# Bias-then-mix kernel: stores begun on SyncE in 4-tile pieces, three loads of x a region, bias units of one tile

## Chip, cores and metric

One core of one Trainium2 chip. The metric is the device time of one execution in microseconds (us), all engines and transfers included. Engines are named as in the profile: PE (TensorE matmul), PEld (its weight load), DVE (VectorE), ACT (ScalarE), POOL (GpSimd), SP (SyncE). "SPq" and "ACTq" are the DMA-issuing instructions of SP and ACT.

## The reference, cut to what matters

```python
# x: (1, 16 heads, 1024 rows t, 1024 columns s), float32
rel  = tril(t - s)                                   # distance, 0 above the diagonal
nd   = log(|c*rel| + 1) / (log(|c*max(t, threshold)| + 1) + EPS)
h    = relu(nd[..., None] * W1[0] + b1)              # 32 hidden values for each (t, s)
y    = x + (h @ W2 + b2)                             # a bias for each head, t, s
out[n,t,s] = sum over m of y[m,t,s] * (A[t][m,n] + B[s][m,n])
# A[t] = w + I + two rank-one terms of qw1, qw2 + diag(qdd): one 16x16 matrix for each row
# B[s] = two rank-one terms of kw1, kw2 + diag(kdd): one 16x16 matrix for each column
```

## The kernel before, in words

x and out are 67 MB each and cross the DMA once each. The 128 partitions hold 16 heads of 8 blocks of 128 columns. A **tile** is 8 rows (all heads, all columns, 512 KB); there are 128. A **region** is a stretch of tiles that is worked on together: region 0 has 8 tiles, regions 1 to 10 have 12 each. Three SBUF areas ("homes") of 13 tile slots take turns: one holds y of region k, one x of region k+1 while it becomes y, one the mixed output of region k, which is stored and then gives its place to x of region k+2.

A region k runs through 16 **column steps** (C = 0 to 15; each mixes 8 columns of every block over all rows of the region with B, `b_columns`, line 750, 64-row weights in 4 places of the array) and then one **row step** for each tile T (`a_rows`, line 735, with A). Steps are numbered s = 0 to 15 and 16 to 27. The matmul results go to one of two PSUM buffers, `main`. In column steps ACT empties the even ones and DVE the odd ones into the mixed home (`take_b`, lines 534 and 636, three copies each; in region 0 ACT takes all). In row steps DVE adds the tile to what lies there (`finish_tile`, line 647). Two fp32 records of the profile are one matmul.

The **bias** of region k+1 is made during region k, at the steps that `BIAS_STEPS` lists. Before, a unit is 16 rows (two tiles): ACT makes `hidden` (line 516) in pieces of 4 blocks, four activations of up to 512 columns for each piece, into a ring of two pieces; PE multiplies it with W2 (`bias_unit`, line 766, 32x32 places, 512 columns, as many output quadrants as lie below the diagonal: 1 for rows 0 to 255, up to 4 for the last 256) into the four PSUM banks of `bias`, which exist once; DVE adds the bias to x, tile by tile, at the unit's step and the next (`add_bias`, line 663, two halves of 512 columns, after a wait for the load of x). Units of a 12-tile region stand at steps 3, 9, 15, 18, 21 and 24. A unit with three or four quadrants is two pieces, the whole ring, so its successor's activations wait until PE has used it (line 512). PE waits in turn for all `hidden` of a unit, and for `y_ready` of the tile before.

Engines run their own program in order, written out by hand; semaphores join them. What sets the order of the DMAs:
- **Stores** (`store_block`, line 313): a region of 12 tiles is stored in pieces of 2, 3, 3 and 4 tiles. Of the 8 blocks of a piece ACT begins four, two at each of two steps behind the last tile of the piece (`portions_at`, line 549 on), and SP the other four.
- **Loads of x** (`load_x`, line 359): pieces of 1, 3, 3, 3 and 2 tiles, 8 DMAs each, all on SP. A piece waits (in SP's program, `out_done`) until the stores that free its slots have landed. Pieces 0, 1 and 2 of region k+2 stand at T = 6, 9 and 11 of region k, the last two behind them, ahead of everything of region k+1.
- **A matrices** (`load_mats_a`, line 367): 4 DMAs for 32 rows, on SP at every fourth tile; POOL spreads them (line 453) after a wait for PE's row steps.

A row of a block is 128 columns of 4 bytes, so x and out move in runs of 512 bytes.

Of the kernel before, what the change touches and what calls it, by code (L numbers as in the profile page):

```python
# [46 lines left out]
BIAS_ROWS = 16  # L47
BIAS_TILES = BIAS_ROWS // ROWS
BIAS_UNITS = S // BIAS_ROWS
SLOT_ROWS = BIAS_ROWS // SLOTS  # L50
PIECE_BLOCKS = 4
PIECE = PIECE_BLOCKS * SLOT_ROWS * W
# [13 lines left out]
def build(nc, x, W1, b1, W2, b2, c, L_mult, init_L, qw1, qw2, kw1, kw2, qdd, kdd, w, out):  # L66
# [5 lines left out]
    with ExitStack() as ctx:  # L72
# [16 lines left out]
        hidden = sb("hidden", [P, RING, PIECE])  # L89
        log_table = sb("log_table", [P, TABLE])  # L90
        row_scale = sb("row_scale", [P, BIAS_UNITS * SLOT_ROWS])
# [64 lines left out]
        def quadrants_of(v):  # L156
            return v * BIAS_ROWS // (QB * W) + 1

        def pieces_of(v):

            blocks = QB * quadrants_of(v)
            return [(b, min(b + PIECE_BLOCKS, blocks)) for b in range(0, blocks, PIECE_BLOCKS)]

        def piece_index(v, i):
            return sum(len(pieces_of(w)) for w in range(v)) + i

        def unit_of_piece(h):
            return max(v for v in range(BIAS_UNITS) if piece_index(v, 0) <= h)

        def hidden_rows(v, i):  # L170
            return hidden[:, piece_index(v, i) % RING, :].rearrange("p (b j s) -> p b j s", j=SLOT_ROWS, s=W)

# [19 lines left out]
        def bias_step(k, n):  # L192

            return BIAS_STEPS[REGION_TILES[k]][n]

        def bias_unit_at(k, s):
            if k + 1 < REGIONS:
                for n in range(REGION_TILES[k + 1] // BIAS_TILES):
                    if bias_step(k, n) == s:
                        return n  # L200
            return None

        def bias_tile_at(k, s):

            n, before = bias_unit_at(k, s), bias_unit_at(k, s - 1)
            if n is not None:
                return n * BIAS_TILES
            return before * BIAS_TILES + 1 if before is not None else None

        def first_unit(k):  # L210
            return FIRST_TILE[k] // BIAS_TILES

        def hidden_parts(v):
            return [(i, j) for i in range(len(pieces_of(v))) for j in range(SLOT_ROWS)]

        def hidden_parts_at(k, s):

            if k + 1 == REGIONS:
                return []
            found = []  # L220
            for n in range(REGION_TILES[k + 1] // BIAS_TILES):
                begun = bias_step(k, n - 1) if n else bias_step(k, 0) - 2
                room = bias_step(k, n) - begun
                parts = hidden_parts(first_unit(k + 1) + n)
                for x, part in enumerate(parts):
                    if begun + x * room // len(parts) == s:
                        found.append((first_unit(k + 1) + n, part))
            return found
# [90 lines left out]
        def portions_at(k, s):  # L319

            found = []
            for r, step in ((k - 1, s + REGION_TILES[k - 1] if k else -1), (k, s - COL_TILES)):
                if r < 0:
                    continue
                for i in range(len(store_pieces(r))):
                    p = step - piece_start(store_pieces(r), i + 1)
                    if 0 <= p < len(PORTIONS):
                        found.append((r, i, p))
            return found

# [13 lines left out]
        def _(sp):  # L344
# [7 lines left out]
            def load_x(k, i):  # L352
                T, n = piece_start(load_pieces(k), i), load_pieces(k)[i]
                if k >= 2 and T + 1 < REGION_TILES[k - 2]:
                    left = piece_of(store_pieces(k - 2), min(T + n, REGION_TILES[k - 2] - 1))
                    sp.wait_ge(out_done[left], times(store_pieces, left, k - 2) * PER_PIECE)
# [126 lines left out]
        def _(act):  # L483
# [20 lines left out]
            def make_hidden(v, part):  # L504
# [14 lines left out]
                if j == SLOT_ROWS - 1:  # L519
                    made.then_inc(hidden_ready, 1)  # L520
# [289 lines left out]
```

## Time and profile before

| | |
|---|---|
| median of 3 runs | 829.97 us (827.63 to 835.9) |
| the profiled execution | 834.87 us; its span, first to last instruction, 833.1 us |
| mean granted TensorE clock | 0.868 of full |
| busy share of the span | PE 70%, DVE 58%, ACT 48%, POOL 19% |
| DMA | 148.37 MB, mean 178 GB/s |

How to read it: times in the rows are us from the span's start unless marked ns. "x32" behind a row is the number of instructions that it merges. The number in square brackets is idle time of that engine just before, and what ended it. The DMA share is the mean busy share of the core's 16 DMA engines. A releaser is inferred from semaphores. The start of a region is read from PE's first column matmuls (a merged row of `mats_b` matmuls right after the last of `mats_a`).

### The profile page before, as it was taken

The page shows a single profiled execution, that of the slowest core. Times are in us where ns is not written, and L with a number is a line of the kernel's source. Part 1 is how long each engine was busy: PE and PEld are TensorE (multiplying, and loading weights), DVE is VectorE, ACT ScalarE, POOL GpSimd, SP SyncE. Part 2 cuts the span into 40 slices and gives each one's busy share as a digit, 9 for nine tenths or more (in the row PEclk, how much of TensorE's full clock was granted, in tenths as well). Part 3 has the DMA queues.
Part 4 walks back from the last instruction along what each step waited for, and adds up shares of the span by engine and source line. Part 5 has one row for each costly group of instructions (what it writes and reads, how often), then busy time and mean ns, then how long its engine had stood idle before and what let it go on. Part 6 is the DMA issues. An engine that isn't in the chain of part 4 may idle for free. (4 is left out here: it accounts for less than half of the span.)

```text
span 833.1 us, 27560 instructions
## 1 busy us (share of the span) xinstructions
PE 581.9 (70%) x12336; PEld 429.0 (51%) x12336; DVE 484.6 (58%) x648; ACT 399.0 (48%) x683; POOL 158.0 (19%) x156
## 2 busy tenths in 40 slices
PE   0556853884896598389569858955974795779683
PEld 0133632663574366167446636834762474357583
DVE  5482633782684577268366746826673475467463
ACT  3548341415523442454385366457537573574310
POOL 1092410130031023003102200400220031003020
PEclk9758985996897799789799989978997799799797
DMA  6978689579879969887986997898599768868739
GB/s 125 212 174 156 156 173 201 123 187 209 186 181 201 198 146 200 183 181 181 225 203 139 201 224 168 184 211 184 135 208 208 156 143 203 184 151 175 143 73 232
DMA packets 298914, 148.37 MB, mean 178 GB/s; under 512 B 30252, under 2 KB 294572, under 8 KB 298668
## 3 DMA queue, kind: packets, MB, share of 16 engines
q1 hardware_dynamic: 229360, 113.03, 61.7%
q10 hardware_dynamic: 69436, 33.58, 17.5%
q8 instruction: 97, 1.59, 0.9%
q14 instruction: 21, 0.17, 0.1%
HBM read 77.34 MB, written 69.21 MB: 176 GB/s over the span
## 5 line engine op out<-in xcount | busy, mean ns | idle before, releaser
L516 ACT ACTIVATE hidden<-log_table,b_col,row_scale 128x512 f32<-128x512 f32 (+1 forms) x384 | 258.0, 734 | 152.6 <-PE bias L766 87.0
L663 DVE SCALAR_TENSOR_TENSOR homes<-bias,b_col,homes 128x512 f32<-128x512 f32 x256 | 180.1, 746 | 205.3 <-PE bias L766 159.3
L750 PE MATMUL main<-homes,mats_b 64*64 64x96 f32 (+1 forms) x5632 | 174.5, 274 | 137.6 <-DVE homes L636 65.6
L735 PEld LDWEIGHTS main<-homes,mats_a 64*64 64x64 f32 x4096 | 231.4, 132 | 35.7 <-issue 29.0
L453 POOL TENSOR_TENSOR mats_a<-mats_in,own_block 128x512 f32<-128x512 f32 x128 | 130.6, 1042 | 617.3 <-PE main L735 601.9
L750 PEld LDWEIGHTS main<-homes,mats_b 64*64 64x64 f32 x5632 | 148.0, 154 | 188.0 <-DVE homes L636 73.7
L534 ACT ACTIVATE homes<-main 64x384 f32<-64x384 f32 (+3 forms) x288 | 134.2, 466 | 229.1 <-PE main L750 209.0
L735 PE MATMUL main<-homes,mats_a 64*64 64x128 f32 x4096 | 241.9, 273 | 0.6 <-issue 0.3
L766 PE MATMUL bias<-hidden,w_blocks 32*32 32x512 f32 x2560 | 166.7, 719 | 88.0 <-ACT hidden L516 71.0
L636 DVE COPY homes<-main 64x384 f32<-64x384 f32 (+1 forms) x240 | 133.2, 555 | 98.0 <-PE main L750 95.8
L647 DVE TENSOR_TENSOR homes<-main,homes 128x1024 f32<-128x1024 f32 x128 | 154.2, 1221 | 25.7 <-PE main L735 25.6
L766 PEld LDWEIGHTS bias<-hidden,w_blocks 32*32 32x32 f32 x2560 | 45.0, 114 | 152.0 <-issue 130.1
L453 POOL TENSOR_TENSOR mats_b<-homes,own_block 128x512 f32<-128x512 f32 x16 | 24.3, 1554 | 38.6 <-DMA homes<-b_mats 38.6
L700 PE MATMUL bias<-relu_b,w_blocks 32*32 32x1 f32 x16 | 0.4, 191 | 12.1 <-DVE w_blocks L619 12.1
L335 DVE TENSOR_TENSOR homes<-mats_in 128x2048 f32<-128x2048 f32 x3 | 8.4, 2826 | 0.0
L700 PEld LDWEIGHTS bias<-relu_b,w_blocks 32*32 32x32 f32 x16 | 0.3, 144 | 12.1 <-issue 12.1
L543 ACT ACTIVATE bias<-zero_col,const_col 32x2048 f32<-32x2048 f32 (+1 forms) x2 | 3.9, 1964 | 5.5 <-DVE const_col L629 5.5
L692 PEld LDWEIGHTS main<-homes 128*128 128x128 f32 x32 | 4.3, 163 | 3.1 <-DVE homes L609 1.7
L495 ACT ACT_TABLE_LOAD x1 | 1.3, 1283 | 7.5 <-issue 7.5
L692 PE MATMUL main<-homes 128*128 128x128 f32 x32 | 4.7, 311 | 0.0
L526 ACT ACTIVATE homes<-main 128x1024 f32<-128x1024 f32 x2 | 1.9, 1023 | 4.0 <-PE main L692 4.0
L607 DVE TENSOR_TENSOR homes<-homes 128x2048 f32<-128x2048 f32 x1 | 3.0, 3014 | 0.0
(32 smaller groups left out, 21.7 us busy)
## 6 DMA issues: line engine op xcount, KB each, us to landing
homes<-in_x SPq DMA_DIRECT2D x248, 192.0 KB, 6.2
out_mixed<-homes ACTq DMA_DIRECT2D x88, 192.0 KB
out_mixed<-homes SPq DMA_DIRECT2D x88, 192.0 KB
homes<-in_x SPq DMA_DIRECT2D x80, 128.0 KB, 4.4
out_mixed<-homes ACTq DMA_DIRECT2D x36, 256.0 KB, 6.9
out_mixed<-homes SPq DMA_DIRECT2D x36, 256.0 KB, 6.2
mats_in<-a_mats SPq DMA_DIRECT2D x128, 64.0 KB, 3.4
out_mixed<-homes SPq DMA_DIRECT2D x48, 128.0 KB, 3.9
```

Of the source, the lines that this page charges most:

```text
L335: return eng.tensor_tensor(dst.rearrange("p (b m n) -> p b m n", b=BLOCKS, m=H), u.unsqueeze(3).to_broadcast(shape), v.unsqueeze(2).to_bro ...
L453: return nc.gpsimd.tensor_tensor(sums.rearrange("p e (n b) -> p e n b", b=QB), rows.rearrange("p n e -> p e n").unsqueeze(3).to_broadcast( ...
L516: made = nc.scalar.activation(hidden_rows(v, i)[:, 0:end_block - first_block, j, :], logs.rearrange("p (b s) -> p b s", s=W), ACT.Relu, bi ...
L534: copy = nc.scalar.activation(mixed_columns(into, k, C, part), column_sums(of, k, C, part), ACT.Copy)
L543: fill = nc.scalar.activation(bias[into].rearrange("p q s -> p (q s)"), zero_col[into].to_broadcast([into.stop - into.start, SLOTS * BANK] ...
L636: copy = dve.tensor_copy(mixed_columns(into, k, C, part), column_sums(of, k, C, part))
L647: dve.tensor_tensor(at, main[:, i % 2, :], at, ALU.add).then_inc(main_taken[i % 2], 1)
L663: add = dve.scalar_tensor_tensor(out=y_rows(whole, k, T, b), in0=falling(u, b), scalar=b2_col[:, 0:1], in1=x_rows(whole, k, T, b), op0=ALU ...
L692: mm = pe.transpose(main[:, i % 2, b * P:(b + 1) * P], comp[part][:, at:at + P], ident)
L735: mm = pe.matmul(main[of_group(g), i % 2, j * W:(j + 1) * W], a_weights(g, w, part * ROWS + j), y_row(k, T, g, j), start=True, stop=True)
L750: mm = pe.matmul(main[into, i % 2, j * W:j * W + REGION_TILES[k] * ROWS], b_weights(g, C * ROWS + j), y_column(k, g, C * ROWS + j), start= ...
L766: mm = pe.matmul(bias[of_quadrant(into), q, :], w2_blocks[of_quadrant(q), b, :], rows, start=b == 0, stop=b == QB - 1)
```

## The change

- Stores: pieces of 4 tiles (8-tile region: 4, 4; 12-tile: 4, 4, 4). All 8 blocks of a piece are begun on SP, in one go, as soon as the piece's last tile is finished. Only the last region keeps its six pieces (2, 3, 3, 2, 1, 1) shared by SP and ACT.
- Loads of x: 3 pieces of 3, 4 and 5 tiles. In SP's program those of region k+2 stand behind the stores of region k: the first behind the second store, the other two behind the third.
- Bias: a unit is one tile (8 rows). Its `hidden` is two activations of all blocks at once (256 to 1024 columns), the ring holds two tiles, the matmuls have 256 columns instead of 512 and there are as many of them for a tile as before for two. In a 12-tile region the tiles stand at steps 4, 8, 12, 15 and then 16, 17, 18, 20, 21, 22, 23, 24, each with its own addition on DVE at the same step.

SP's program for a region of 12 tiles is then: at T=3 store piece 0, A chunk; at T=7 store piece 1, A chunk, x piece 0 of region k+2; at T=11 store piece 2, A chunk, x pieces 1 and 2.

```diff
-STORE_PIECES = {8: (2, 3, 3), 12: (2, 3, 3, 4)}
+STORE_PIECES = {8: (4, 4), 12: (4, 4, 4)}
-LOAD_PIECES = {8: (1, 3, 4), 12: (1, 3, 3, 3, 2)}
-X_PIECES = 5
+LOAD_PIECES = {8: (1, 3, 4), 12: (3, 4, 5)}
+X_PIECES = 3
-BIAS_STEPS = {8: (3, 8, 12, 15, 18, 20), 12: (3, 9, 15, 18, 21, 24)}
+BIAS_STEPS = {8: (2, 4, 6, 8, 10, 12, 14, 16, 17, 18, 20, 21), 12: (4, 8, 12, 15, 16, 17, 18, 20, 21, 22, 23, 24)}
-BIAS_ROWS = 16
...
-SLOT_ROWS = BIAS_ROWS // SLOTS
-PIECE_BLOCKS = 4
-PIECE = PIECE_BLOCKS * SLOT_ROWS * W
+SLOT_ROWS = ROWS // SLOTS
+HIDDEN = BLOCKS * SLOT_ROWS * W
 RING = 2
...
+            for T, step in enumerate(bias_steps(k)):
+                begun = bias_steps(k)[T - 1] if T else step - 2
+                for j in range(SLOT_ROWS):
+                    if begun + j * (step - begun) // SLOT_ROWS == s:
+                        found.append((tile_of(k + 1, T), j))
             return found
...
+        def is_shared(k, i):
+
+            return k + 1 == REGIONS
...
+        def stores_before(k, i):
+
+            T, n = piece_start(load_pieces(k), i), load_pieces(k)[i]
+            if k < 2 or T + 1 >= REGION_TILES[k - 2]:
+                return None
+            return piece_of(store_pieces(k - 2), min(T + n, REGION_TILES[k - 2] - 1))
...
-            def store_upper(k, i):
+            def store_piece(k, i):
                 taken, count = emptied(a_tile(k, piece_start(store_pieces(k), i + 1) - 1))
                 sp.wait_ge(taken, count)
-                for b in BLOCK_ORDER[sum(PORTIONS):]:
+                for b in BLOCK_ORDER[sum(PORTIONS):] if is_shared(k, i) else BLOCK_ORDER:
                     store_block(sp, k, i, b).then_inc(out_done[i], DMA)
...
-            for i in range(3):
+            for i in range(X_PIECES - 1):
                 load_x(1, i)
             save_mats("a")
-            load_x(1, 3)
             sp.wait_ge(mats_out["a"], 2 * DMA)
             for v in range(A_RING):
                 load_mats_a(v)
-            load_x(1, 4)
-            loaded = [3, X_PIECES] + [0] * (REGIONS - 2)
+            load_x(1, X_PIECES - 1)
             for k in range(REGIONS):
-
-                while k + 1 < REGIONS and loaded[k + 1] < X_PIECES:
-                    load_x(k + 1, loaded[k + 1])
-                    loaded[k + 1] += 1
+                pieces, loaded = store_pieces(k), 0
                 for T in range(REGION_TILES[k]):
+                    stored = [i for i in range(len(pieces)) if T == piece_start(pieces, i + 1) - 1]
+                    for i in stored:
+                        store_piece(k, i)
                     v = chunk_behind(tile_of(k, T))
                     if v is not None:
                         load_mats_a(v)
-                    for i in range(len(store_pieces(k))):
-                        if T == piece_start(store_pieces(k), i + 1) - 1 - (i == 3 and k < REGIONS - 1):
-                            store_upper(k, i)
-                    if k + 2 < REGIONS and T in (6, 9, 11):
-                        load_x(k + 2, loaded[k + 2])
-                        loaded[k + 2] += 1
+                    for i in stored:
+
+                        while k + 2 < REGIONS and loaded < X_PIECES and (
+                                i + 1 == len(pieces) or stores_before(k + 2, loaded) < i):
+                            load_x(k + 2, loaded)
+                            loaded += 1
...
+            def make_hidden(u, j):
+                blocks = QB * quadrants_of(u)
...
+                if j == 0 and u >= RING:
+                    act.wait_ge(hidden_used, u - RING + 1)
+                at = u * ROWS + j - (blocks * W - 1) + BEFORE
+                made = nc.scalar.activation(hidden_rows(u)[:, 0:blocks, j, :],
...
-            def falling(u, b):
-                at = (u % BIAS_TILES) * 2 + b
-                return bass.AP(bias, at * BANK + W - 1, [[SLOTS * BANK, P], [W, SLOT_ROWS], [-1, W]])
+            def falling(b):
+                return bass.AP(bias, b * W + W - 1, [[SLOTS * BANK, P], [BANK, SLOTS], [-1, W]])
...
-                dve.wait_ge(hidden_used, u // BIAS_TILES + 1)
+                dve.wait_ge(hidden_used, u + 1)
...
+            def bias_tile(u):
+                if u:
+                    pe.wait_ge(y_ready, u)
+                pe.wait_ge(hidden_ready, u + 1)
                 for b in range(QB):
                     for q in range(SLOTS):
+                        for into in range(quadrants_of(u)):
+                            at = QB * quadrants_of(u) - 1 - (QB * into + b)
+                            mm = pe.matmul(bias[of_quadrant(into), q, 0:SLOT_ROWS * W], w2_blocks[of_quadrant(q), b, :],
+                                           hidden_rows(u)[of_quadrant(q), at], start=b == 0, stop=b == QB - 1)
                 mm.then_inc(hidden_used, 1)
```

## Rows read from the trace of the kernel before

**Rows 1.** Waits: engine, tile, line <- releaser: us in total, times, longest us
```profile
ACT hidden L516 <- PE bias L766: 87.0, 27, 4.5
...
PE bias L766 <- ACT hidden L516: 71.0, 31, 8.3
...
DVE homes L663 <- DMA homes<-in_x: 40.2, 7, 14.5
```

**Rows 2.** Busy time by stage: PE, PEld, DVE, ACT, POOL busy; PEclk, DMA share, GB/s
```profile
183.20:225.20 42.00, 24.68 (x608) 16.38 (x608) 19.90 (x33) 22.59 (x39) 2.05 (x2) 0.76 0.93 198
...
695.20:739.90 44.70, 24.55 (x704) 15.24 (x704) 20.00 (x34) 29.00 (x48) 2.04 (x2) 0.85 0.90 207
739.90:771.20 31.30, 29.48 (x582) 24.24 (x576) 23.80 (x28) 17.38 (x24) 10.21 (x10) 1.00 0.66 144
```

**Rows 3.** Timeline of PE, regions 9 and 10: start us, us, work [idle before <-releaser]
```profile
699.70 1.56 PE L750 MATMUL main<-homes,mats_b 64*64 64x96 f32 x64 [2.33 <-ACT homes L534]
708.71 3.75 PE L766 MATMUL bias<-hidden,w_blocks 32*32 32x512 f32 x64 [7.46 <-ACT hidden L516]
...
723.02 4.08 PE L766 MATMUL bias<-hidden,w_blocks 32*32 32x512 f32 x64 [2.14 <-ACT hidden L516]
...
739.93 5.66 PE L735 MATMUL main<-homes,mats_a 64*64 64x128 f32 x96
745.93 2.34 PE L766 MATMUL bias<-hidden,w_blocks 32*32 32x512 f32 x64 [0.35 <-ACT hidden L516]
...
771.37 0.90 PE L750 MATMUL main<-homes,mats_b 64*64 64x96 f32 x32 [0.24 <-DVE homes L647]
...
797.95 22.25 PE L735 MATMUL main<-homes,mats_a 64*64 64x128 f32 x384
```

**Rows 4.** Timeline of ACT, regions 0 and 9
```profile
85.67 2.08 ACT L516 ACTIVATE hidden<-log_table,b_col,row_scale 128x256 f32<-128x256 f32 x4
...
689.27 8.84 ACTq L313 DMA_DIRECT2D out_mixed<-homes  x4
...
704.16 1.46 ACT L534 ACTIVATE homes<-main 128x384 f32<-128x384 f32 x3
...
740.03 5.75 ACT L516 ACTIVATE hidden<-log_table,b_col,row_scale 128x512 f32<-128x512 f32 x8 [2.52 <-PE bias L766]
```

**Rows 5.** Timeline of DVE, region 9
```profile
720.95 1.69 DVE L636 COPY homes<-main 128x384 f32<-128x384 f32 x3 [1.02 <-PE main L750]
727.23 2.91 DVE L663 SCALAR_TENSOR_TENSOR homes<-bias,b_col,homes 128x512 f32<-128x512 f32 x4 [4.58 <-PE bias L766]
...
742.10 1.23 DVE L647 TENSOR_TENSOR homes<-main,homes 128x1024 f32<-128x1024 f32 x1 [0.56 <-PE main L735]
```

**Rows 6.** Timeline of PE, regions 0 to 4: other widths and region starts
```profile
61.39 0.70 PE L750 MATMUL main<-homes,mats_b 64*64 64x64 f32 x32 [0.24 <-ACT homes L526]
...
106.44 0.90 PE L750 MATMUL main<-homes,mats_b 64*64 64x96 f32 x32 [0.24 <-DVE homes L647]
...
168.09 1.92 PE L766 MATMUL bias<-hidden,w_blocks 32*32 32x512 f32 x16
...
183.28 0.90 PE L750 MATMUL main<-homes,mats_b 64*64 64x96 f32 x32 [0.24 <-DVE homes L647]
...
230.90 1.95 PE L766 MATMUL bias<-hidden,w_blocks 32*32 32x512 f32 x32
...
384.35 2.21 PE L766 MATMUL bias<-hidden,w_blocks 32*32 32x512 f32 x48
```

**Rows 7.** The page's DMA queues: packets, MB, share of 16 engines' span
```profile
q1 hardware_dynamic: 229360, 113.03, 61.7%
q10 hardware_dynamic: 69436, 33.58, 17.5%
```

**Rows 8.** Timeline of SyncE's issues, three loads of x in a row
```profile
492.30 19.37 SPq L359 DMA_DIRECT2D homes<-in_x  x24
```

**Rows 9.** The loads of x (line 359), from issue to landing
```profile
DMA to landing us min/median/max: 3.4/5.8/9.0
```

More of the change, by code:

```diff
@@ L154, in tile_of, with quadrants_of, hidden_rows @@
             return FIRST_TILE[k] + T
[L156 to L171, printed above, removed]
+        def quadrants_of(u):
+            return u * ROWS // (QB * W) + 1
+        def hidden_rows(u):
+            return hidden[:, u % RING, :].rearrange("p (b j s) -> p b j s", j=SLOT_ROWS, s=W)
         def turned_tile(part, half):
@@ L190, in emptied, with bias_steps @@
             return main_taken[i % 2], i // 2 + 1
[L192 to L201, printed above, removed]
-        def bias_tile_at(k, s):
[L205 to L214, printed above, removed]
+        def bias_steps(k):
+            return BIAS_STEPS[REGION_TILES[k]] if k + 1 < REGIONS else ()
+        def bias_tile_at(k, s):
+            return bias_steps(k).index(s) if s in bias_steps(k) else None
         def hidden_parts_at(k, s):
-            if k + 1 == REGIONS:
-                return []
             found = []
[L221 to L227, printed above, removed]
+            for T, step in enumerate(bias_steps(k)):
[3 more added lines that the diff above has]
+                        found.append((tile_of(k + 1, T), j))
             return found
@@ L317, in portion_blocks, with portions_at @@
             return BLOCK_ORDER[sum(PORTIONS[:p]):sum(PORTIONS[:p + 1])]
-        def portions_at(k, s):
+        def is_shared(k, i):
+            return k + 1 == REGIONS
+        def portions_at(k, step):
             found = []
[L322 to L328, printed above, removed]
-            return found
+            for i in range(len(store_pieces(k))):
+                p = step - piece_start(store_pieces(k), i + 1)
+                if is_shared(k, i) and 0 <= p < len(PORTIONS):
+                    found.append((i, p))
+            return found
+        def stores_before(k, i):
[3 more added lines that the diff above has]
+            return piece_of(store_pieces(k - 2), min(T + n, REGION_TILES[k - 2] - 1))
         def rank_one(eng, part, i, dst):
@@ L353, in load_x @@
                 T, n = piece_start(load_pieces(k), i), load_pieces(k)[i]
-                if k >= 2 and T + 1 < REGION_TILES[k - 2]:
-                    left = piece_of(store_pieces(k - 2), min(T + n, REGION_TILES[k - 2] - 1))
+                left = stores_before(k, i)
+                if left is not None:
                     sp.wait_ge(out_done[left], times(store_pieces, left, k - 2) * PER_PIECE)
@@ L535, in take_b @@
                 copy.then_inc(main_taken[b_tile(k, C) % 2], 1)
-            for v in range(REGION_TILES[0] // BIAS_TILES):
-                for part in hidden_parts(v):
-                    make_hidden(v, part)
-                if v == 0:
+            for u in range(REGION_TILES[0]):
+                for j in range(SLOT_ROWS):
+                    make_hidden(u, j)
+                if u == 0:
                     act.wait_ge(const_bias_read, 1)
@@ L546, in _ @@
                     fill.then_inc(const_filled, 1)
-                if v == 1:
+                if u == 2:
                     take_turned("b")
@@ L550, in _ @@
                 for s in steps(k):
[L551 to L556 removed]
+                    for i, p in portions_at(k, s - COL_TILES):
+                        store_portion(k, i, p)
                     if s == TURN_AT and k == 0:
@@ L560, in _ @@
                         take_b(k, s)
-                    for v, part in hidden_parts_at(k, s):
-                        make_hidden(v, part)
-            r = REGIONS - 1
-            for i in range(len(store_pieces(r))):
-                for p in range(len(PORTIONS)):
-                    if piece_start(store_pieces(REGIONS - 1), i + 1) + p >= REGION_TILES[REGIONS - 1]:
-                        if p == 0:
-                            taken, count = emptied(a_tile(REGIONS - 1, piece_start(store_pieces(REGIONS - 1), i + 1) - 1))
-                            act.wait_ge(taken, count)
-                        for b in portion_blocks(p):
-                            store_block(act, REGIONS - 1, i, b).then_inc(out_done[i], DMA)
+                    for u, j in hidden_parts_at(k, s):
+                        make_hidden(u, j)
+            for step in range(REGION_TILES[REGIONS - 1], REGION_TILES[REGIONS - 1] + len(PORTIONS)):
+                for i, p in portions_at(REGIONS - 1, step):
+                    store_portion(REGIONS - 1, i, p)
         @block.vector
```

62 lines of the change are left out of this document (21 added, 41 removed).

## The prediction

> **What bounds the kernel now.** I read the waits first: ACT's `hidden` waits on PE's bias matmuls and these on `hidden`, 87.0 and 71.0 us [rows 1]. That is one loop: a unit with three or four quadrants fills the whole ring, so ACT and PE work in turn. Next the stages: in region 9 the column steps take 44.5 us, in which PE is busy 24.5 and ACT 29.0, and the row steps 31.3, in which PE is busy 29.5 [rows 2]. The column steps are thus where time is lost, the row steps are PE's. PE's timeline shows the loss: 7.46 and 2.14 us idle before bias units, a third wait like the second, units of 3.75 and 4.08 us behind such waits against 2.34 in the row steps, and 2.33 us at the start, when ACT is late [rows 3] because it sits in 8.84 us of DMA issues [rows 4]. Last the DMA: both queues' packets take 61.7 + 17.5 = 79.2% of 833.1 us for 146.6 MB, that is 4.50 us/MB or 222 GB/s at full share [rows 7]. The column steps run at 198 and 207 GB/s with a share of 0.90 to 0.93, the row steps at 144 [rows 2]. So the DMA is the second bound, close behind, and the question is how soon it becomes the first.
>
> **Prices.** A row tile is 5.66/3 or 22.25/12, 1.87 us [rows 3]. A column step is 0.90 on PE [rows 3]; a pair goes round in DVE's 1.69 plus the 1.02 in which DVE waits for the same buffer, 2.71 [rows 5]. ACT's three copies are 1.46 [rows 4], DVE's addition of one tile 1.41 to 1.46 (2.91 for two) and `finish_tile` 1.23 [rows 5].
>
> **`hidden`.** 256 columns cost 2.08/4 = 0.52, 512 cost 5.75/8 = 0.72 [rows 4]; 0.20 for 256 columns gives 0.92 for 768 and 1.12 for 1024, so 2.24 us a tile at most against 2.88 for half a unit before. Bounds of the 1024: 0.72 and twice that. At 1.12 ACT's column pair is 1.46 + 1.12 = 2.58, inside DVE's 2.71; at 1.44 it would be 2.90, and 8 pairs cost 1.5 us more. In the row steps ACT needs 2.24 for a step of 3.3 on PE, and the ring of two tiles lets it run ahead. So the loop of [rows 1] goes, and 0 of `hidden` is left on the path. ACT's issues fall from 180 stores to 24, so its late start in each column stage goes too.
>
> **Bias matmuls with 256 columns.** The trace has none. A unit of 512 columns is 1.92, 1.95, 2.21 and 2.34 us for 16, 32, 48 and 64 records [rows 3, 6]. Lower end: half. Upper end: no cheaper than 512, since the count stays. Between them: 32 records of the column steps take 0.90 with 96 columns and 0.70 with 64 [rows 3, 6], so 0.30 of 32 records does not depend on columns, 9 ns a record. With that a tile of 64 records is 0.6 + (2.34 - 0.6)/2 = 1.47; for 16, 32, 48: 1.03, 1.12, 1.32. I take 1.0, 1.1, 1.3, 1.45 for one to four quadrants. Two tiles cost PE up to 0.6 more than the unit did.
>
> **Column stage after.** Start and first pair 1.1, 7 pairs x 2.71 = 19.0, the last step 0.9: 21.0. Three tiles (steps 4, 8, 12) each put an addition of 1.41 into DVE's round, with some wait for PE about 1.5: 4.5. Bias of T=3 behind step 15: 1.1. Sum 26.6; I take 27 at two quadrants, 27.4 at three, 28 at four, where 40 to 48 stand now.
>
> **Row stage after.** 12 x 1.87 + 8 tiles x 1.1 = 31.2 at two quadrants, 32.8 at three, 34 at four (DVE's 1.23 + 1.41 = 2.64 fits into a step of 2.95). Without a DMA wait a region would take 58.5 to 62.5 us.
>
> **The DMA after.** A region moves 12 x 0.524 MB twice and 3 x 0.262 of A: 13.37 MB, at 4.50 us/MB 60.2 us. One store piece is 9.4, an A chunk 1.2, the loads 7.1, 9.4, 11.8. All of it is in SP's order now. SP can issue that fast: 24 loads, 4.72 MB, in 19.37 us, 244 GB/s [rows 8]. What counts is where x lands. Let e be the region's end; its T=7 is finished at e - 8.3 (four more tiles and a bias; two quadrants). Behind that come store 1, A, x piece 0: e - 8.3 + 9.5 + 1.2 + 7.1 = e + 9.5, and about 3 for landing (3.4 is the shortest of issue to landing [rows 9]): e + 12.5. The next region wants this x for its T=0 behind step 4, at e + 7.6. So DVE waits 4.9 us, every region, with the empty column copies of DVE queued behind this wait, and PE behind them; another 1.5 goes as PE comes back slow (a unit behind a wait costs 3.75 against 2.34 [rows 3]). Piece 1 lands at e + 9.5 + 9.5 + 1.2 + 9.5 + 3 = e + 32.7, wanted at step 15, e + 33; piece 2 at e + 44.5, wanted at step 20, e + 47. They fit, barely. The queue is then empty for some 4 us until the next store at T=3.
> A region of two quadrants: 0.2 + 27 + 4.9 + 1.5 + 31.1 = 64.7; three: 65.9; four: 67.4 (the wait shrinks to 4 as the rows lengthen). 13.37 MB in 64.7 us is 207 GB/s, what region 9's column stage moves now [rows 2].
>
> A rule of the Trainium skill bears on the stores (DMA: Bandwidth & Descriptors, section "Issuing engines are not separate DMA queues"): transfers begun on several engines run on the same 16 DMA engines, so a second issuing engine saves only issue time. By it the move to SP neither gains nor loses bandwidth. The same page (section "Queues, rings and completion order") says that a DMA engine takes packets from its queues in turn; with one queue a load gets no turn ahead of a store. The trace has SP's loads at full rate alone, but no stretch with all stores on SP, so it does not settle that; the 4.9 us already hold the full delay.
>
> **Regions 0, 1 and 10.** Region 0 keeps its setup; its tail gains 2 us from five single tiles and a later x piece. Region 1 takes 183.28 - 106.44 = 76.8 us now [rows 6] with its wait for x, the longest of 14.5 [rows 1]. After, region 0's two stores follow its T=3 and T=7, so x piece 0 of region 2 lands at about 131 (T=7 at 109, then 1.3 behind store 0, 9.5, 1.2, 7.1, 3) and is wanted at 116: 15 us again, and region 1 ends at 183 as before. Regions 2 to 9 run from 183.3 to 771.4, 588.1 us [rows 3, 6]; after: 3 x 64.7 + 2 x 65.9 + 3 x 67.4 = 528. Region 10 has no bias; its column stage, 797.95 - 771.37 = 26.6 [rows 3], falls to 8 x 2.71 + 1 = 22.7 since ACT is not late; row steps and last stores stay. Sum: 833.1 - 60 - 4 = 769 us of span. The profiled execution was 834.87 for 833.1, so 771 for this one; the median 829.97 is 0.994 of it: **766 us**.
>
> **Rivals.**
> 1. *The DMA does not bind.* If the packets got shorter with traffic of one kind at a time, x would be there at step 4. For it: three loads at 244 GB/s [rows 8]. Against: 4.50 us/MB over the run [rows 7]. Regions of 58.3, 60 and 62.5 make 482, less 10 in region 1: about 712. The Trainium skill (DMA: Bandwidth & Descriptors, section "Specifications") gives a limit of some 358 GB/s for each core from HBM; at that, an estimate, 13.37 MB would take 37 us. No run here shows such a rate.
> 2. *256 columns cost what 512 cost.* Then bias tiles are 1.9 to 2.3, a region has 12 x 0.8 more on PE, of which the wait at step 4 gives back 2.4: 7 us x 8, about 822. Against: the slope between 64 and 96 columns [rows 3, 6].
> 3. *Slower: one queue, one order.* Stores and loads take turns in a single queue, and x piece 0 waits behind a whole store. At a rate r a region is 13.37 MB/r and 4 us of empty queue; the present 73.5 is reached at 192 GB/s. For it: 198 GB/s in region 2's column stage at a share of 0.93 [rows 2]. Against: 222 at full share [rows 7]. At 181 GB/s, 6% below that, a region is 78, 8 x 78 = 624, the whole 862.
>
> **Numbers.** Forecast 0.74, with its own range 741 to 804: the DMA between 235 and 200 GB/s moves a region's traffic by 3.3 down and 6.6 up, of which I let half show since PE is close behind; bias tiles and `hidden` towards their bounds are 1.5 either way; 8 regions x -3.2 and +4.8. Rival 1: 0.08; rival 2: 0.08, half of it within 1%; rival 3: 0.10, nearly all slower by over 1%. One per cent is about what a measurement of this kernel can tell. So faster 0.74 + 0.08 + 0.04 = 0.86, same 0.05, slower 0.09. The range 735 to 815 leaves out most of rival 1 and 3 and part of 2.
>
> **What would show it.** Right: ACT `hidden` and PE bias hardly wait for each other; bias matmuls near 1.0 to 1.5 us a tile; column stages of 30 to 34 us with one DVE wait of some 5 us on x at step 4; DMA share above 0.9 throughout regions 2 to 9, at 205 to 215 GB/s. Wrong: DVE waits on x also at steps 15 and 20; row steps above 35 us; a DMA rate below 195 GB/s with a share near 1.

## The result and the profile after

The change makes the kernel slower: 888.62 us against 832.41 in the same comparison, a ratio of 1.069 (95% interval 1.063 to 1.075). The profiled execution took 886.17 us for a span of 884.4. Medians in this document are over all executions of a kernel; ratios and their intervals leave out those in a second, slower state, in which the profiles of the kernel before and of `e12_pairs_from_2` were taken.

The page of the kernel after (engine totals; queues: packets, MB, share of 16 engines' span; chain by engine):

```profile
PE 617.0 (70%) x14896; PEld 476.2 (54%) x14896; DVE 490.9 (56%) x648; ACT 367.9 (42%) x555; POOL 158.6 (18%) x156
...
q1 hardware_dynamic: 287408, 143.44, 79.9%
q10 hardware_dynamic: 7548, 3.16, 1.6%
q8 instruction: 117, 1.92, 1.0%
...
PE 41%; SPq 25%; DVE 15%; DMA 9%; issue 7%; ACT 1%; ACTq 1%; POOL 0%; DVEq 0%; POOLq 0%
```

The stores have moved: q10 (ACT's, [rows 7]) is nearly empty. The chain runs through SP's DMA issues (SPq, 25%), and 7% of it is "issue", an engine that waits for nothing the profile shows. The waits of the same kernel (engine, tile, line <- releaser: us in total, times, longest us):

```profile
ACT hidden L480 <- PE bias L724: 176.3, 68, 10.7
...
DVE homes L624 <- DMA homes<-in_x: 111.4, 14, 18.8
...
PE bias L724 <- issue: 23.6, 17, 2.9
...
PE main L711 <- issue: 20.1, 11, 4.4
PE bias L724 <- ACT hidden L480: 18.4, 16, 1.7
PE main L696 <- issue: 16.9, 9, 5.4
```

Against [rows 1] PE's wait for `hidden` fell from 71.0 to 18.4: that loop is gone (ACT's 176.3 is ACT ahead, with nothing to do). DVE's wait for x rose from 40.2 to 111.4. New is PE idle by "issue", 60.6 us in the three rows. By stage, regions 2 and 9, column steps and row steps (PE, PEld, DVE, ACT, POOL busy; PEclk, DMA share, GB/s), the whole region 2, and a stretch across the start of region 2:

```profile
196.90:237.00 40.10, 21.46 (x646) 16.04 (x642) 18.43 (x31) 19.38 (x34) 2.04 (x2) 0.79 0.92 192
237.00:276.90 39.90, 33.38 (x644) 26.60 (x638) 26.02 (x30) 10.64 (x14) 10.19 (x10) 0.91 0.78 157
751.40:786.50 35.10, 22.28 (x774) 16.76 (x770) 18.50 (x31) 23.54 (x34) 2.04 (x2) 0.90 0.83 189
786.50:827.60 41.10, 38.73 (x903) 30.90 (x899) 26.06 (x29) 16.62 (x14) 10.19 (x10) 0.92 0.86 167
196.90:276.90 80.00, 54.84 (x1282) 42.64 (x1280) 44.45 (x60) 30.02 (x48) 12.23 (x12) 0.85 0.85 175
...
184.70:223.20 38.50, 25.10 (x594) 20.08 (x596) 20.22 (x28) 12.24 (x22) 6.12 (x6) 0.82 0.99 212
```

Column stages are shorter than in [rows 2] (42.0 and 44.7), row stages longer: 41.1 in region 9, where 31.3 stood. The DMA at a share of 0.99 moves 212 GB/s; over the whole of region 2 it is 175 at 0.85. Region by region, worked out from the two traces (from one region's first column matmul to the next one's; "x" is DVE's waits for x, "issue" PE's idle by "issue" over 0.3 us):

```
region          0    1    2    3    4    5    6    7    8    9   10
before        61.3 76.8 70.3 72.8 73.8 71.2 69.6 76.1 78.3 76.0 48.8
after         71.4 76.7 80.1 72.4 75.6 78.2 76.3 85.4 86.5 76.2 43.7
  x, step 4    -   18.8 10.3  9.5 12.8  8.9  8.4  8.6  6.7  4.4  -
  x, later    11.6  -    -    4.3  2.9  2.8  -    -    -    1.4  -
  issue        2.8  1.7  9.2  3.3  3.3  4.8  5.7 14.9 10.1  4.6  0
```

The timeline of PE shows both losses (start us, us, work [idle before <-releaser]):

```profile
184.67 1.06 PE L724 MATMUL bias<-hidden,w_blocks 32*32 32x256 f32 x16
185.66 2.03 PE L696 MATMUL main<-homes,mats_a 64*64 64x128 f32 x32
187.62 1.07 PE L724 MATMUL bias<-hidden,w_blocks 32*32 32x256 f32 x16
...
217.33 2.84 PE L711 MATMUL main<-homes,mats_b 64*64 64x96 f32 x64 [11.08 <-DVE homes L598]
...
226.81 1.09 PE L724 MATMUL bias<-hidden,w_blocks 32*32 32x256 f32 x32
228.03 0.55 PE L711 MATMUL main<-homes,mats_b 64*64 64x96 f32 x10
231.31 1.39 PE L711 MATMUL main<-homes,mats_b 64*64 64x96 f32 x54 [2.73 <-issue]
...
237.04 0.78 PE L696 MATMUL main<-homes,mats_a 64*64 64x128 f32 x9
243.18 2.82 PE L696 MATMUL main<-homes,mats_a 64*64 64x128 f32 x23 [5.35 <-issue]
...
716.53 3.68 PE L696 MATMUL main<-homes,mats_a 64*64 64x128 f32 x32
...
725.78 1.50 PE L724 MATMUL bias<-hidden,w_blocks 32*32 32x256 f32 x64
727.21 2.03 PE L696 MATMUL main<-homes,mats_a 64*64 64x128 f32 x32
```

At 217 PE comes back after 11.08 us: DVE sat behind x. At 231 and at 243 it stops in the middle of a merged group, after 10 of 64 records and after 9 of 32, where it has nothing to wait for. After such a stop it can also be slow for a while: the 32 records at 716.53, right behind a stop of 2.95 us, took 3.68 us, those at 727.21 took 2.03. That is the clock: the granted clock is 0.50 (1.2 GHz) from 716.5 to 720.2 and 1.00 (2.4 GHz) from 727.2 to 729.3. The DVE and SP timelines of the same kernel:

```profile
101.78 1.41 DVE L624 SCALAR_TENSOR_TENSOR homes<-bias,b_col,homes 128x512 f32<-128x512 f32 x2 [11.58 <-DMA homes<-in_x]
...
214.26 1.41 DVE L624 SCALAR_TENSOR_TENSOR homes<-bias,b_col,homes 128x512 f32<-128x512 f32 x2 [10.32 <-DMA homes<-in_x]
215.59 1.68 DVE L598 COPY homes<-main 128x384 f32<-128x384 f32 x3
```

```profile
187.47 3.50 SPq L337 DMA_DIRECT2D mats_in<-a_mats  x4
191.01 7.99 SPq L276 DMA_DIRECT2D out_mixed<-homes  x8
199.05 3.54 SPq L337 DMA_DIRECT2D mats_in<-a_mats  x4
202.63 6.05 SPq L329 DMA_DIRECT2D homes<-in_x  x8
208.72 8.75 SPq L276 DMA_DIRECT2D out_mixed<-homes  x8
217.51 3.33 SPq L337 DMA_DIRECT2D mats_in<-a_mats  x4
220.88 26.55 SPq L329 DMA_DIRECT2D homes<-in_x  x16
```

SP is in its issues without a break from 187 to 247. The first x piece is issued by 208.7 and its tile is added at 214.3.

**What the "issue" stops are.** The 27 stops over 0.5 us sum to 56.6 us (before: 4 and 5.7). Count PE's own instructions in order, that is matmuls, weight loads and the few semaphore and drain instructions between them. Each of the 27 stops then ends at number 193 or 194 of a block of 256, and 1.2 to 1.7 us after a packet of queue q8, "instruction", has ended. The list has 2 x 14,896 + 288 = 30,080 instructions, that is 117.5 blocks of 256, and q8 carried 117 packets of 1.92 MB/117 = 16 KB. Before it was 24,896, 97.3 blocks and 97 packets:

```profile
q8 instruction: 97, 1.59, 0.9%
```

In the traces of the kernel before and of all the experiments every such stop ends at 193 or 194 as well. At each of the 27 exactly as many packets had ended as PE had gone through whole blocks; none was there ahead. So q8 is PE's instruction stream, and PE ran dry: at the stop ahead of 243.18, the packet began at 240.65 and ended at 241.57; the one before had ended 11.8 us earlier. The Trainium skill (Runtime: NRT & Kernel Launch, section "Instruction fetch mechanics") says that an engine's instructions come in blocks of 256 by a DMA queue of its sequencer, and that crossing a block is mostly hidden. The traces agree on the block. That it is hidden holds for most of the 117 blocks here, but 27 of them cost 56.6 us.

### The profile page after: what moved, and what is told of

It reads as the page before. It is cut to its first block, busy times and chain, and to the rows that moved or that the text cites. A ratio compares the mean times of both kernels' runs of the same rounds, so it can differ in the third digit from the quotient of the medians.

```text
span 884.4 us, 32376 instructions
## 1 busy us (share of the span) xinstructions
PE 617.0 (70%) x14896; PEld 476.2 (54%) x14896; DVE 490.9 (56%) x648; ACT 367.9 (42%) x555; POOL 158.6 (18%) x156
## 3 DMA queue, kind: packets, MB, share of 16 engines
q8 instruction: 117, 1.92, 1.0%
## 4 chain that ended last, share of the span: by engine, by line
PE 41%; SPq 25%; DVE 15%; DMA 9%; issue 7%; ACT 1%; ACTq 1%; POOL 0%; DVEq 0%; POOLq 0%
PE main L696 20%; PE bias L724 14%; SPq L276 11%; DMA homes<-in_x 8%; SPq L329 8%; PE main L711 7%; DVE homes L598 6%; SPq L337 6%; DVE homes L624 5%; DVE homes L609 1%; DVE homes L305 1%; DMA a_mats<-homes 1%; PE main L653 1%; DVE homes L566 1%; POOL mats_a L421 0%
## 5 line engine op out<-in xcount | busy, mean ns | idle before, releaser
L480 ACT ACTIVATE hidden<-log_table,b_col,row_scale 128x256 f32<-128x256 f32 (+3 forms) x256 | 224.3, 915 | 179.6 <-PE bias L724 176.3
L624 DVE SCALAR_TENSOR_TENSOR homes<-bias,b_col,homes 128x512 f32<-128x512 f32 x256 | 180.3, 746 | 204.1 <-DMA homes<-in_x 111.4
L696 PE MATMUL main<-homes,mats_a 64*64 64x128 f32 x4096 | 271.4, 285 | 17.1 <-issue 16.9
L696 PEld LDWEIGHTS main<-homes,mats_a 64*64 64x64 f32 x4096 | 246.3, 139 | 59.0 <-issue 53.2
L711 PE MATMUL main<-homes,mats_b 64*64 64x96 f32 (+1 forms) x5632 | 166.6, 265 | 148.0 <-DVE homes L598 117.0
L724 PE MATMUL bias<-hidden,w_blocks 32*32 32x256 f32 x5120 | 191.4, 429 | 71.3 <-issue 23.6
L711 PEld LDWEIGHTS main<-homes,mats_b 64*64 64x64 f32 x5632 | 141.7, 147 | 182.4 <-DVE homes L598 128.3
L609 DVE TENSOR_TENSOR homes<-main,homes 128x1024 f32<-128x1024 f32 x128 | 156.7, 1224 | 93.9 <-PE main L696 93.9
L724 PEld LDWEIGHTS bias<-hidden,w_blocks 32*32 32x32 f32 x5120 | 83.6, 111 | 134.5 <-issue 80.3
L653 PE MATMUL main<-homes 128*128 128x128 f32 x32 | 6.5, 386 | 5.7 <-DVE homes L571 5.7
L498 ACT ACTIVATE mats_a<-main 128x1024 f32<-128x1024 f32 x2 | 1.9, 1021 | 3.3 <-PE main L653 3.3
```

The lines of the kernel that those rows point to most:

```text
L480: made = nc.scalar.activation(hidden_rows(u)[:, 0:blocks, j, :], log_table[:, at:at + blocks * W].rearrange("p (b s) -> p b s", s=W), ACT. ...
L609: dve.tensor_tensor(at, main[:, i % 2, :], at, ALU.add).then_inc(main_taken[i % 2], 1)
L624: add = dve.scalar_tensor_tensor(out=y_rows(whole, k, T, b), in0=falling(b), scalar=b2_col[:, 0:1], in1=x_rows(whole, k, T, b), op0=ALU.ad ...
L696: mm = pe.matmul(main[of_group(g), i % 2, j * W:(j + 1) * W], a_weights(g, w, part * ROWS + j), y_row(k, T, g, j), start=True, stop=True)
L711: mm = pe.matmul(main[into, i % 2, j * W:j * W + REGION_TILES[k] * ROWS], b_weights(g, C * ROWS + j), y_column(k, g, C * ROWS + j), start= ...
L724: mm = pe.matmul(bias[of_quadrant(into), q, 0:SLOT_ROWS * W], w2_blocks[of_quadrant(q), b, :], hidden_rows(u)[of_quadrant(q), at], start=b ...
```

## The experiments

**The two halves apart.** `e1_bias_alone` is the kernel after with stores and loads as before; `e2_transfers_alone` is the kernel before with stores and loads as after.

```diff
--- e1, against the kernel after
-STORE_PIECES = {8: (4, 4), 12: (4, 4, 4)}
+STORE_PIECES = {8: (2, 3, 3), 12: (2, 3, 3, 4)}
-LOAD_PIECES = {8: (1, 3, 4), 12: (3, 4, 5)}
-X_PIECES = 3
+LOAD_PIECES = {8: (1, 3, 4), 12: (1, 3, 3, 3, 2)}
+X_PIECES = 5
...
+                    if k + 2 < REGIONS and T in (6, 9, 11):
+                        load_x(k + 2, loaded[k + 2])
```

> The bias in units of one tile at the new steps, with the stores and loads of the kernel before. Theory A (late x: in the changed kernel DVE waits 111.4 us for x against 40.2, because pieces of x stand behind whole stores in SyncE's order): the waits fall back to 40 us or less, column stages shrink by some 10 us a region, and the time is 770 to 800 us. Theory B (PE's instructions: in the changed kernel PE stands 57 us in 27 gaps of over 0.5 us that the profile calls issue, against 6 us in 4; the doubled bias matmuls run its instruction supply dry while the DMA is busy): 30 us or more of these gaps stay, with slow matmuls behind each, and the time is 810 to 850.

Measured: 816.81 us, 0.974 (0.965 to 0.984). Its waits for x and its "issue" rows, and its stages of region 2:

```profile
PE main L709 <- issue: 21.7, 15, 4.3
...
DVE homes L622 <- DMA homes<-in_x: 17.5, 5, 9.2
...
PE bias L722 <- issue: 11.3, 14, 2.7
...
PE main L694 <- issue: 6.8, 7, 2.4
```

```profile
179.80:210.00 30.20, 19.73 (x648) 15.39 (x645) 17.71 (x30) 19.43 (x34) 2.04 (x2) 0.89 0.95 210
210.00:242.20 32.20, 31.61 (x644) 25.40 (x638) 26.57 (x31) 10.65 (x14) 10.21 (x10) 1.00 0.97 224
```

The waits for x fall, as the first theory has it, and the stops stay, as the second has it. The bias half is a gain, and where x and instructions are hardly late it is near the forecast's 58.5 (without a wait) to 64.7: region 2 takes 30.2 + 32.2 = 62.4 us, with the DMA at 210 to 224 GB/s. But the late regions, with three and four quadrants, take 69.6 to 79.6, and 36.1 us of stops at block ends are there without the new transfers.

> The new stores and loads of x with the bias units of two tiles of the kernel before, whose tiles 2 and 3 are wanted at step 9 already. Theory A: DVE waits for x 110 us or more, and the time is 890 or more, slower than the kernel before by all of the loss and what the bias part would have gained. Theory B: issue gaps of PE fall to under 15 us and the time is under 870.

Measured: 903.23, 1.087 (1.078 to 1.095). DVE waits 196.9 us for x, some 10 at step 3 and 10 at step 9 of each region; stops at block ends are 9.6. The loss is the transfers' half.

**Which part of the transfers.** `e7_old_pieces_on_sp` is e1 with all stores issued by SP; `e11_loads_alone` is e1 with the new loads; `e13_big_loads_early` has the new sizes at T = 6, 9, 11; `e14_small_loads_late` the old sizes in the new places.

```diff
--- e7, against e1
-                for b in BLOCK_ORDER[sum(PORTIONS):]:
+                for b in BLOCK_ORDER[sum(PORTIONS):] if k == REGIONS - 1 else BLOCK_ORDER:
...
--- e11, against e1
-LOAD_PIECES = {8: (1, 3, 4), 12: (1, 3, 3, 3, 2)}
+LOAD_PIECES = {8: (1, 3, 4), 12: (3, 4, 5)}
...
+                    upto = X_PIECES if T == REGION_TILES[k] - 1 else 1 if T == 7 else 0
--- e13, against e11
-                    upto = X_PIECES if T == REGION_TILES[k] - 1 else 1 if T == 7 else 0
+                    upto = X_PIECES if T == REGION_TILES[k] - 1 else sum(T >= at for at in (6, 9))
--- e14, against e11
-LOAD_PIECES = {8: (1, 3, 4), 12: (3, 4, 5)}
+LOAD_PIECES = {8: (1, 3, 4), 12: (1, 3, 3, 3, 2)}
...
```

> The bias-alone kernel, with the stores of all regions but the last begun on SyncE alone, in the old pieces of 2, 3, 3 and 4 tiles and with the old loads of x. If the loss of the changed transfers is in the pieces and their order, not in the queue: within 1.5% of the bias-alone kernel, 805 to 829. If one queue for all costs: 840 or more.

> The bias-alone kernel, stores shared and in the old pieces, but x loaded in pieces of 3, 4 and 5 tiles at T=7 and T=11, as in the changed kernel. If the loss is in the loads' sizes and places: DVE waits for x 80 us or more against 17, and the time is 850 or more. If it is in the stores' 4-tile pieces on SyncE: under 835, waits under 50 us.

> The bias-alone kernel with x in pieces of 3, 4 and 5 tiles at the old places T=6, 9 and 11. If the places are the cause: the waits for x fall under 35 us, issue gaps to some 40, and the time to 815 to 835, as with the old pieces. If the sizes are: 870 or more.

> The bias-alone kernel with the old five pieces of x (1, 3, 3, 3, 2 tiles), but in the changed kernel's places: the first at T=7, the other four at T=11. If the places are the cause: 870 or more, with DVE waiting for x 70 us or more, at step 8 where piece 2 is wanted. If the sizes are: under 835.

Measured (ratio to the kernel before; the last two columns from the profiled executions, stops over 0.5 us at block ends):

```
                      median   ratio (95%)             DVE waits on x   PE stops
e1                    816.81   0.974 (0.965 to 0.984)       17.5          36.1
e7 stores all on SP   841.64   1.015 (1.011 to 1.020)      110.2          31.7
e14 places alone      852.60   1.029 (1.020 to 1.038)       98.5          21.5
e13 sizes alone       874.85   1.060 (1.051 to 1.069)       25.7          75.0
e11 both, loads only  901.96   1.085 (1.076 to 1.094)       72.8          68.7
after                 888.62   1.069 (1.063 to 1.075)      111.4          56.6
```

Two costs come apart. Late places, and stores in front of loads on one engine, cost waits for x. Big pieces at the old, early places cost hardly any such wait, but PE runs out of instructions. (e14's 852.6 lies between the two times expected for it.) The waits of e13 and of e14:

```profile
PE main L705 <- issue: 33.3, 15, 5.5
...
PE bias L718 <- issue: 26.3, 13, 3.9
...
DVE homes L618 <- DMA homes<-in_x: 25.7, 4, 9.8
...
PE main L690 <- issue: 17.5, 10, 4.1
```

```profile
PE main L706 <- DVE homes L593: 107.1, 29, 11.1
DVE homes L619 <- DMA homes<-in_x: 98.5, 15, 11.0
```

The new loads alone account for the whole loss, and the columns don't simply add. A kernel that waits for x may ask for instructions less often; that is not shown. On one engine or two: the Trainium skill (DMA: Bandwidth & Descriptors, section "Issuing engines are not separate DMA queues") says that a second issuing engine saves only issue time. The traces nearly agree: at full share the DMA moves 217 GB/s in e7, 222 in e1. In e7 SP has all the issues, and x waits behind stores that ACT used to begin: DVE's waits for x go from 17.5 to 110.2 us, and the median is 25 us above e1's.

**Attempts to mend the loads.** `e5_first_x_small`: x in pieces of 1, 2, 4, 5. `e10_after_x_before_mats`: region 1's last x piece ahead of the wait for the A matrices. `e15_loads_halved`: each DMA of x split into two of half the rows. `e4_stores_shared`: the pieces of 4 tiles shared by ACT and SP. All against the kernel after.

```diff
--- e5
-LOAD_PIECES = {8: (1, 3, 4), 12: (3, 4, 5)}
+LOAD_PIECES = {8: (1, 3, 4), 12: (1, 2, 4, 5)}
...
--- e10
             save_mats("a")
+            load_x(1, X_PIECES - 1)
             sp.wait_ge(mats_out["a"], 2 * DMA)
...
-            load_x(1, X_PIECES - 1)
--- e15
...
+                half = n * ROWS // 2
                 for b in BLOCK_ORDER:
...
+                    for h in range(2):
...
+                                     x[0, :, t0 + h * half:t0 + (h + 1) * half, b * W:(b + 1) * W]).then_inc(x_in[i], DMA)
--- e4
-            return k + 1 == REGIONS
+            return True
...
```

> The changed kernel with x in pieces of 1, 2, 4 and 5 tiles instead of 3, 4 and 5, in the same places of SyncE's order. Theory A by the order (DVE's wait at step 4 is for the whole first piece behind store 1): one tile lands 3 to 5 us sooner than three, the wait at step 4 falls from 4.4 to 12.8 us a region to 2 to 8, and the time to 850 to 875. If the wait has to do with the rate alone, or only moves to step 8: 880 or more.

> The changed kernel with the last x piece of region 1 begun ahead of the wait for the A matrices in the setup, as its tiles 7 to 9 were before. DVE's wait of 11.6 us in region 0's row steps goes, region 0 falls from 71 to 58 to 63 us, the other regions stay, and the time is 873 to 881. If the piece is late for lack of DMA rate: the wait stays over 6 us.

> The changed kernel with every DMA of x split into two of half the rows, in the same order; bytes and waits stay, SyncE has 24 more issues a region. If the size of a DMA makes x land late and PE's instructions wait: the issue gaps fall from 57 to under 35 us and the time to 850 to 875. If not: within 12 us of the changed kernel, 875 to 900.

> The changed kernel with the stores of all regions shared by SyncE and ScalarE, four blocks each, as before, in the same pieces of 4 tiles. If one queue for all costs DMA rate or delays x behind stores (theory A by the queue): faster than the changed kernel by 20 us or more, 840 to 865. If it is the sizes and places of the pieces: within 10 us of it, 878 to 898.

Measured, in one execution each: 894.68, 894.58, 933.57 and 921.8 us. None is a gain, and only e5 lies in a range that was expected for it, the one of no gain. In e5 the wait at step 4 of regions 2 to 4 fell to 5.6 to 7.8, and another of 9.2 to 12.2 came in the row steps, for the last piece. In e10 the wait in region 0's row steps is gone (its row steps fell from 33.3 to 21.5), and its column stage grew from 38.0 to 46.8, since the A matrices now come late: PE's first row step waits 7.67 us for them. In e15 the stops fell from 56.6 to 31.3, but the waits for x grew from 111.4 to 193.6: a piece of 3 tiles that SP issued in 6.05 us took it 11.09:

```profile
220.90 11.09 SPq L331 DMA_DIRECT2D homes<-in_x  x16
```

In e4 the stores go back to two engines, and ACT stands in their issues in the column steps (6 issues, 11.72 us, ahead of its copies); x waits are 91.9, stops 67.6. Each of these orders of SP's DMAs mended one thing and made another late.

**Instructions, or bytes?** `e3_little_x`: the kernel after, with one row in eight of x loaded from region 4 on. `e6_two_quadrants` (e1) and `e9_after_two_quadrants` (after): no more than two quadrants on PE.

```diff
--- e3
+                rows = n * ROWS if k < 4 else n
--- e6, e9
-                        for into in range(quadrants_of(u)):
+                        for into in range(min(quadrants_of(u), 2)):
```

> The changed kernel, but the loads of x of regions 4 to 10 carry one row in eight of their rows (the rest of x is left out), so the DMA is never full there and x is never late. If the forecast's prices for PE, DVE and ACT hold, regions 4 to 8 last 58 to 64 us. Theory B in the form that a full DMA delays PE's instructions: the issue gaps vanish there (under 2 us a region). If PE's supply is too slow by itself: gaps of 4 us or more a region stay.

> The bias-alone kernel, with at most two of the up to four output quadrants computed on PE (the bias of the others is left out); ACT, DVE and all transfers stay. Theory B (PE's instruction supply): regions 7 to 9, with 79.6, 79.5 and 73.8 us in the bias-alone kernel, fall to 62 to 68 and their issue gaps from 5 to 9 us to under 3. If the gaps come from the DMA load alone: they stay, and the regions lose only the matmuls' own 0.4 us a tile, 70 to 75 us.

> The changed kernel with at most two of the up to four output quadrants of the bias computed on PE (the others are left out), transfers as changed. If PE's instruction supply costs what its gaps show: the gaps fall from 57 us to about 25, regions 7 to 9 from 85, 87 and 76 us to 70 to 76, where the wait for x of some 9 us a region holds them, and the time to 840 to 855. If the late x alone sets the pace: 865 or more.

Measured: 796.3, 776.08 and 861.19 us. In e3 regions 4 to 7 take 64.5, 65.5, 65.5 and 67.7, near the forecast's 64.7 to 67.4 with its wait for x; 58 to 64 were expected without one. DVE still waits 4.3 to 6.0 at step 4 there, with little x to move: what is left is x standing behind a store and an A chunk, and its landing. Stops in regions 4 to 9 fall from 43.4 to 16.4 us, so the load on the DMA has a part in them. Regions 8 and 9 keep 7.8 and 4.8 us of them at a mean of 111 and 115 GB/s, but the mean hides what stands around them. In the 4 us before each of the packets that ended their seven stops over 0.5 us the DMA's share is 0.92 to 1.23 (packets counted where they start), against 0.62 and 0.58 over the two regions. A full DMA is not needed for every stop: those of 1.40 us at 278.46 and of 0.81 us at 537.84 come behind shares of 0.15 and 0.16.

In e6 regions 7 and 8 take 134.3 us where e1 needs 159.0:

```profile
508.60:642.90 134.30, 111.72 (x2566) 86.71 (x2564) 88.81 (x120) 78.22 (x96) 24.49 (x24) 0.87 0.90 200
```

```profile
512.90:671.90 159.00, 128.01 (x3269) 98.87 (x3268) 89.64 (x120) 78.61 (x96) 24.49 (x24) 0.86 0.79 180
```

(e6 above, e1 below.) Of these 24.7 us, 16.3 are work that PE no longer has, and 8.4 are idle time; over the run its stops fall from 36.1 to 24.5. In e9, 27 us faster than after and between the two times expected for it, stops fall from 56.6 to 40.5 and waits for x rise to 130.0.

**Fewer instructions for the same bias.** `e8_pairs_late` is e1 with units of two tiles, 512 columns and half the matmuls for regions 6 to 10; `e12_pairs_from_2` does it from region 2 on.

```diff
+PAIR_STEPS = (3, 9, 15, 18, 21, 24)
+PAIRED = 6
...
+                            if n == 2:
+                                rows = hidden[of_quadrant(q), :, at * SLOT_ROWS * W:(at + 1) * SLOT_ROWS * W]
...
+                            mm = pe.matmul(bias[of_quadrant(into), q, 0:n * SLOT_ROWS * W], w2_blocks[of_quadrant(q), b, :],
```

> The bias-alone kernel, in which from region 6 on (three and four quadrants) PE takes two tiles with one set of matmuls of 512 columns, at the steps 3, 9, 15, 18, 21 and 24 of the kernel before; hidden stays two activations a tile. Theory B: PE has 768 to 1024 instructions fewer per such region, the gaps in regions 5 to 9 fall under 2 us, these regions last 69 to 75 us where the bias-alone kernel has 70 to 80, and the time is 783 to 805. If the gaps stay: 810 or more.

> The kernel with pairs of tiles on PE from region 2 on instead of region 6. If one-tile units gain only where instructions are few (one and two quadrants): regions 1 to 4 go from 71, 67, 63, 69 to 68 to 74 us each and the time is 805 to 822, between this and the kernel before. If the gain of the bias part is in the two activations a tile and not in the one-tile units: 795 to 808, as with pairs from region 6 on.

Measured: e8 803.29 us, 0.963 (0.954 to 0.972), the fastest of all that compute everything, though its interval overlaps e1's. For e12 it is 828.78, 0.986 (0.976 to 0.996), in the median above both ranges expected for it. Stops are 21.2 and 7.9 us against e1's 36.1, with 104 and 98 packets of instructions against 117. Units of one tile pay where a tile has one or two quadrants: regions 1 to 4 take 261.9 us in e1, 269.5 in e8, which has the same units there, and 289.9 in e12. Units of two pay in regions 7 and 8, where tiles have three or four: 71.4 and 69.8 us in e8, 79.6 and 79.5 in e1. In regions 5, 6 and 9 e8 differs from e1 by -1.5, +3.7 and +2.3 us, no more than the two differ in regions 2 to 4, where they are alike.

## Why the prediction was wrong

**Right: the prices of the bias.** `hidden`, by form, of the kernel after (busy, mean ns of one):

```profile
L480 ACT ACTIVATE hidden<-log_table,b_col,row_scale 128x1024 f32<-128x1024 f32 x64 | 76.4, 1235 | 55.0 <-PE bias L724 54.7
L480 ACT ACTIVATE hidden<-log_table,b_col,row_scale 128x768 f32<-128x768 f32 x64 | 62.9, 1022 | 40.0 <-PE bias L724 39.4
```

1.24 and 1.02 us for 1.12 and 0.92. Bias matmuls, start to start in the PE timeline above: 0.99 us for 16 records (184.67 to 185.66) and 1.43 for 64 (725.78 to 727.21), for 1.0 and 1.45. The loop of ACT and PE went, as said. Region 10's column stage is 21.4 us for 22.7. A row tile between bias tiles is 1.96 (185.66 to 187.62) for 1.87, about 1 us a region. Rival 2 is out.

**Wrong: where x lands.** The step that failed is "e - 8.3 + 9.5 + 1.2 + 7.1 = e + 9.5", with about 3 for landing "e + 12.5". At the start of region 2 (e = 196.9) T=7 was done at e - 7.9, near the forecast, but SP was still in the A chunk behind store 0 and began store 1 at e - 5.9. It was through by e + 2.1, with the next A chunk by e + 5.7, x piece 0 by e + 11.8, and its first tile was added at e + 17.4. The A chunk was priced by its bytes, 1.2 us; its four issues hold SP for 3.3 to 3.5 us in the rows above, and two chunks stand ahead of x. (Store and x piece took SP 8.0 and 6.1 us, less than their 9.5 and 7.1.) Landing was taken as about 3, from the shortest time in [rows 9], 3.4 us, which is that of a DMA of 128 KB; it took 5.6 here, and loads of 192, 256 and 320 KB have medians of 5.8, 7.4 and 8.4 us on the page. The row of the first piece's size:

```profile
homes<-in_x SPq DMA_DIRECT2D x88, 192.0 KB, 5.8
```

The wait at step 4 came out at 8.7 us as a mean of regions 2 to 9, against 4.9: 8 x 3.8 = 30 us. Later waits, "they fit, barely", add 11.4.

**Wrong: no term for PE's instructions.** There are as many bias matmuls for a tile as before for two, and the step "Two tiles cost PE up to 0.6 more than the unit did" priced them by PE's time alone. It has no line for the 5,120 matmuls and weight loads more, whose instructions come by DMA. Stops of PE take 55.9 us of regions 2 to 9, besides the slower matmuls behind the longer ones. Row steps, forecast at 31 to 34, are 33.7 to 47.4.

**Wrong: region 0.** It was to grow by 2 us and grew by 10.1. The last x piece of region 1, five tiles behind the A matrices, came 11.6 us late, and e10 shows that ahead of them it is no better.

Waits and stops make 30 + 11 + 56 = 97 of the 102.7 us by which regions 2 to 9 (630.7 for 528) missed. This is no exact account: 10.5 us of the stops lie inside DVE's waits for x and count twice, and the slower matmuls behind stops are not in it. Regions 0 and 1 add 13.6 us, since region 2 begins at 196.9 for 183.3. Of the prediction's own signs of being wrong, row steps above 35 us came, and later waits for x in four regions; a rate below 195 GB/s at a share near 1 did not.

**The rival that came nearest** is the third, slower by one queue and one order, at 862 us and 78 a region with the DMA at 181 GB/s; measured were 78.8 and, in region 2, 175 (share 0.85). Its place, x behind a whole store, is there (after, e7), and its lever, a lower rate of the DMA at full share, is there in part. Taken as the prediction took its 222 GB/s, from the time of both queues' packets, it is 203 after: 81.5% of 884.4 us for 146.6 MB. In e1 it is 222, in e7 217, in e14 214, in e13 216 and in e11 207. But 203 is far from 181, and with a share of 0.86 and 174 GB/s over regions 2 to 9 the DMA itself stood idle at times. How much of the waits for x the slower packets make is not shown. About half of the miss has another cause, which no case contained. Rival 1 is out too: x is not there at step 4. The 244 GB/s of [rows 8], its support, were SP's pace of issue; over the same stretch, 492.3 to 511.7, the DMA moved 206 GB/s.

**Not settled:** why big pieces bring more stops. By size of the loads' DMAs, after, e4, e10, e11 and e13 (192 to 320 KB) have 57 to 75 us, and e1, e7, e14 (up to 192) and e15 (halved) 21 to 36. But e5, most of whose x comes by DMAs of 256 and 320 KB, has 29.4. The trace shows when an instruction packet moves, not when it was asked for.

## What to carry to other kernels

When a change multiplies matmuls, count PE's instructions per microsecond as a stream that shares the DMA, and look at the "issue" rows and the instruction queue before trusting a price in PE time. A transfer is there when its whole piece has landed behind all that its engine issues first: price every issue ahead of it, and take landing from a row of its own size. Test the halves of a combined change apart; here one was worth 2.6% and the other lost more than three times that.

## What the runs showed of the hardware that was not expected

- PE's instructions come in packets of 16 KB, 256 at a time. With 117 of them in 794 to 932 us, PE stood dry for 21 to 75 us, each time until 1.2 to 1.7 us after a packet had ended (in the kernel after). Most of the stops that are left with little x (e3) come behind a full DMA, but one of 1.40 us came behind a share of 0.15.
- Small DMAs cost SP time of their own: the four issues of an A chunk, 64 KB each, held it for 3.3 to 3.5 us in the rows above, while their bytes at 222 GB/s would take 1.2; a piece of 3 tiles in 16 DMAs (e15) held it for 11.09 us, in 8 for 6.05.
